# Softmax sums applied to the probabilities in SBUF, ahead of their transposes, in an AdaLN block with attention and experts

## What is computed

```python
e = jnp.exp(logits - m)
exp_sink = jnp.exp(s - m)
w = e / (jnp.sum(e, axis=-1, keepdims=True) + exp_sink)
out = jnp.einsum('bhmqk,bkhd->bqhmd', w, v).reshape(Bv, Tv, N_HEADS * HEAD_DIM)
return out @ out_w.T + out_b
```

## Time and profile before

| | us |
|---|---|
| median of 3 runs | 1054.87 (1053.17 to 1055.72) |
| profiled execution | 1054.14 |
| its span, first to last instruction | 1052.6 |
| TensorE busy, by matmuls | 957.0 |
| VectorE busy | 752.4 |
| ScalarE busy | 745.2 |
| GpSimd busy | 466.5 |
| mean granted TensorE clock | 0.963 of full speed |

### The profile page before, as it was taken

The page is one execution under the profiler, slowest core; times in us unless marked ns, Lnnn a source line. Parts: engine busy times, 40 slices in busy tenths (PEclk is TensorE's granted clock), DMA queues, the critical chain, the costliest instruction groups (busy, mean ns, idle before and its releaser), DMA issues.

```text
span 1052.6 us, 22639 instructions
## 1 busy us (share of the span) xinstructions
PE 957.0 (91%) x6862; PEld 897.0 (85%) x6862; DVE 752.4 (71%) x2212; ACT 745.2 (71%) x2058; POOL 466.5 (44%) x551
## 2 busy tenths in 40 slices
PE   5689999999899899999999999999997599999991
PEld 3479899989789799988999999999996489999991
DVE  6677887878788467777777777777764756666646
ACT  3368787888788688788878788887885356565541
POOL 4347668768657333433443332222222852222243
PEclk9889999999999899999999999999998699999996
DMA  8789879698467576465556555444302375555313
GB/s 183 176 221 280 219 209 272 209 216 206 116 162 170 160 192 158 114 167 134 136 142 166 132 150 137 116 120 152 81 2 96 115 263 161 175 163 163 104 59 117
DMA packets 146040, 166.09 MB, mean 158 GB/s; under 512 B 79194, under 2 KB 100714, under 8 KB 140800
## 3 DMA queue, kind: packets, MB, share of 16 engines
q1 hardware_dynamic: 129440, 143.58, 51.9%
q0 software_dynamic: 3696, 11.09, 3.3%
q10 hardware_dynamic: 12784, 9.97, 3.1%
HBM read 105.82 MB, written 58.79 MB: 156 GB/s over the span
## 4 chain that ended last, share of the span: by engine, by line
PE 63%; DVE 13%; ACT 9%; issue 8%; DMA 3%; POOL 2%; SPq 1%; ACTq 0%; DVEq 0%; POOLq 0%
PE psO L1107 15%; PE psS L1074 11%; PE psX L1084 9%; PE psY L1123 7%; PE psP L1003 7%; ACT wgt_hi L1340 3%; DVE gated L2094 2%; PE psO L1090 2%; PE psP L1016 2%; PE psP L1033 2%; POOL xg L910 2%; DVE pTl L1776 1%; ACT relu_s L1636 1%; PE psS L1257 1%; PE psX L1257 1%
## 5 line engine op out<-in xcount | busy, mean ns | idle before, releaser
L1372 ACT ACTIVATE pbuf<-pbuf,nmax 128x257 f32<-128x257 f32 (+5 forms) x512 | 264.2, 518 | 45.0 <-DVE nmax L1750 36.7
L1074 PE MATMUL psS<-kT,qE 128*128 128x256 f32 (+3 forms) x1024 | 237.2, 316 | 24.2 <-DVE nmax L1750 13.8
L1776 DVE TENSOR_TENSOR pTl<-psX,pTh 128x512 fp32r<-128x512 f32 x272 | 187.1, 688 | 71.4 <-ACT pTh L1340 70.4
L1340 ACT ACTIVATE pTh<-psX 128x512 fp32r<-128x512 f32 x272 | 160.6, 590 | 58.8 <-PE psO L1107 41.5
L1074 PEld LDWEIGHTS psS<-kT,qE 128*128 128x128 f32 x1024 | 161.2, 192 | 35.7 <-DVE nmax L1750 22.0
L1107 PE MATMUL psO<-pTh,vpad 128*128 128x256 f32 x1088 | 186.3, 293 | 3.3 <-DVE oS L1782 2.1
L814 POOL TENSOR_TENSOR ol<-oS,oh 128x256 fp32r<-128x256 f32 x128 | 94.8, 741 | 201.5 <-ACT oh L1340 197.0
L1084 PE MATMUL psX<-idn,pbuf 128*128 128x128 f32 x1088 | 161.8, 274 | 2.7 <-DVE pTl L1776 2.6
L1107 PEld LDWEIGHTS psO<-pTh,vpad 128*128 128x128 f32 x1088 | 149.7, 189 | 10.6 <-DVE oS L1782 5.5
L1753 DVE CUSTOM_DVE_ANT_0 pbuf<-psS,mcau 128x128 f32<-128x128 f32 (+3 forms) x256 | 123.0, 484 | 24.7 <-PE psS L1074 22.7
L1750 DVE CUSTOM_DVE_ANT_0 pbuf<-psS,mcau 128x257 f32<-128x257 f32 (+1 forms) x256 | 98.8, 387 | 50.3 <-PE psS L1074 47.0
(11 more groups left out here) (294 smaller groups left out, 2359.7 us busy)
## 6 DMA issues: line engine op xcount, KB each, us to landing
qd<-st SPq DMA_DIRECT2D x32, 1024.0 KB, 4.5
qE<-qd SPq DMA_DIRECT2D x128, 256.0 KB, 5.9
mrawV<-in_w_moe SPq DMA_DIRECT2D x32, 384.0 KB, 3.5
mrawB<-in_w_moe SPq DMA_DIRECT2D x32, 384.0 KB, 3.4
kT<-kd SPq DMA_DIRECT2D x64, 128.0 KB, 4.3
kT<-kd SPq DMA_DIRECT2D x32, 256.0 KB, 4.3
kd<-st SPq DMA_DIRECT2D x7, 1024.0 KB, 5.5
xg<-sq ACTq DMA_DIRECT2D x7, 640.0 KB, 6.2
```

Source lines behind the costliest of these rows:

```text
L1074: last = mm(psS[j % 2][:, at:at + n], qE[:, g % 2, j, t * P:(t + 1) * P], kT[:, g % 2, c, k0:k0 + n], start=(c == 0), stop=(c == 1))
L1340: copy = lambda o, i: nc.scalar.activation(o, i, ACT.Copy)
L1372: nc.scalar.activation(pj, pj, ACT.Exp, bias=nmax[:, u % 4, j:j + 1], scale=-1.0, accum_out=sums[:, u % 4, j:j + 1]).then_inc(a_exp, 1)
L1776: V.tensor_tensor(pTl[:, kt % 2, :], psX[kt % 2][:, :], pTh[:, kt % 2, :], ALU.subtract).then_inc(v_pl, 1)
```

## The change

The four heads' probabilities are multiplied with their reciprocals in SBUF, in place in `pbuf`, before TensorE turns them: heads 0 and 1 by one instruction of GpSimd, head 2 on VectorE, head 3 on ScalarE. The first `turn_probs` of a unit waits for all three in place of the exponentials. `spread`, `turn_scale`, `scale_of` and `scale_out` go, and with them `rdenx`, `rS` and `oS`. `oh` is now rounded from `psO` itself, `ol` is taken by VectorE from `psO` too, and `values` of the next unit waits for that. The reciprocals are made one step earlier (`denominator(u - 1)` in step u), the products stand in step u+1 of each engine, and `out_project` comes one step earlier. On GpSimd, `rope_low`, `low_weights`, the product and `rope_sum` now come in this order at the head of a step, ahead of `tables` and `residual`.

```diff
+
+        def heads_of(u):
+
+            n = keys(u) * P
+            step = n + 2 if windowed(u) else n
+            at = PROB[u % TB]
+            return pbuf[:, at:at + 2 * step].rearrange("p (j n) -> p j n", j=2)[:, :, step - n - windowed(u):step - windowed(u)]

...

-            def out_low(u):
-                pool.wait_ge(a_oh, u + 1)
+            def normalize(u):
+
+                pool.wait_ge(v_rden, u + 1)
                 apart(pool)
-                G.tensor_tensor(ol[:, u % 2, :], oS[:, u % 2, :], oh[:, u % 2, :], ALU.subtract).then_inc(g_ol, 1)
-
-            def spread(u):
-
-                pool.wait_ge(v_rden, u + 1)
-                wait(pool, s_rx, u)
-                apart(pool)
-                G.tensor_copy(rdenx[:, :].rearrange("p (h d) -> p h d", h=QM),
-                              rden[:, u % 4, :].unsqueeze(2).broadcast_to([P, QM, HD])).then_inc(g_rx, 1)
+                both = heads_of(u)
+                G.tensor_tensor(both, both, rden[:, u % 4, 0:2].unsqueeze(2).broadcast_to([P, 2, keys(u) * P]), ALU.mult)\
+                 .then_inc(g_norm, 1)

...

             def step(u):
                 seg, r = divmod(u, SEGU)
-                if 0 <= u - 4 < NU:
-                    out_low(u - 4)
+                if turns(u - 1):
+                    rope_low(ahead(u - 1)[:2])
+                if u < NU:
+                    low_weights(u)
+                if 0 <= u - 1 < NU:
+                    normalize(u - 1)
+                if turns(u):
+                    rope_sum(ahead(u)[:2])
                 if seg == 2 and 8 <= r < 20:
                     tables(r - 8)
                 if seg in (1, 2) and 3 <= r < 3 + TB:
                     residual(TB * (seg - 1) + r - 3)
-                if turns(u - 1):
-                    rope_low(ahead(u - 1)[:2])
-                if u < NU:
-                    low_weights(u)
-                if turns(u):
-                    rope_sum(ahead(u)[:2])
-                if 0 <= u - 1 < NU:
-                    spread(u - 1)
...
@@ -1078,22 +1075,18 @@
             def turn_probs(u, k):
                 kt = KT[u] + k + 1
                 if k == 0:
-                    pe.wait_ge(a_exp, QM * (u + 1))
+                    pe.wait_ge(g_norm, u + 1)
+                    pe.wait_ge(v_norm, u + 1)
+                    pe.wait_ge(a_norm, u + 1)
                 wait(pe, v_pl, kt - 2)
                 for j in range(QM):
                     last = turn(psX[kt % 2][:, j * P:(j + 1) * P], probs(u, j)[:, k * P:(k + 1) * P], idn[:, :])
                 last.then_inc(s_X, 1)

-            def turn_scale(u):
-                pe.wait_ge(g_rx, u + 1)
-                for i in range(2):
-                    last = turn(psO[:, (2 + i) * P:(3 + i) * P], rdenx[:, i * P:(i + 1) * P], idn[:, :])
-                last.then_inc(s_rx, 1)
-
             def values(u, k):
                 kt = KT[u] + k + 1
                 if k == 0:
-                    wait(pe, v_os, u)
+                    wait(pe, v_ol, u)
...
@@ -1138,11 +1131,9 @@
                 if u >= 3:
                     values(u - 3, keys(u - 3) - 1)
                 scores(u, 1)
-                if u >= 3:
-                    turn_scale(u - 3)
                 scores(u, 2)
-                if u >= 5:
-                    out_project(u - 5)
+                if u >= 4:
+                    out_project(u - 4)
                 scores(u, 3)
...
                 if nk > 3:
                     turn_probs(u - 2, 3)
-                out_project(u - 5)
+                if u - 4 < NU:
+                    out_project(u - 4)
...

-            def scale_of(u):
-                act.wait_ge(s_rx, u + 1)
-                wait(act, v_os, u - 1)
-                copy(rS[:, u % 2, :], psO[:, 2 * P:4 * P]).then_inc(a_rx, 1)
-
             def out_hi(u):
-                act.wait_ge(v_os, u + 1)
+                act.wait_ge(s_PV, KT[u + 1])
                 wait(act, s_Y, u - 1)
-                copy(oh[:, u % 2, :], oS[:, u % 2, :]).then_inc(a_oh, 1)
+                copy(oh[:, u % 2, :], psO[:, 0:2 * P]).then_inc(a_oh, 1)
+
+            def normalize(u):
+
+                act.wait_ge(v_rden, u + 1)
+                pj = probs(u, QM - 1)
+                nc.scalar.activation(pj, pj, ACT.Copy, scale=rden[:, u % 4, QM - 1:QM]).then_inc(a_norm, 1)

...
                 exp_head(u, 0)
-                if u >= 3:
-                    scale_of(u - 3)
                 if nk > 1:
                     probs_hi(u - 2, 1)
-                if u >= 4:
-                    out_hi(u - 4)
+                if u >= 3:
+                    out_hi(u - 3)
                 exp_head(u, 1)
+                if u >= 1:
+                    normalize(u - 1)
                 exp_head(u, 2)
                 if item and by_scalar(item):
                     high(item)
...
                 if u - 3 < NU:
-                    scale_of(u - 3)
+                    out_hi(u - 3)
                 if now:
                     exp_head(u, 1)
                 if nk > 1:
                     probs_hi(u - 2, 1)
+                if u - 1 < NU:
+                    normalize(u - 1)
                 if now:
                     exp_head(u, 2)
...
                     exp_head(u, 3)
-                if u - 4 < NU:
-                    out_hi(u - 4)
...

-            def scale_out(u):
-                dve.wait_ge(s_PV, KT[u + 1])
-                wait(dve, g_ol, u - 1)
-                dve.wait_ge(a_rx, u + 1)
-                V.tensor_tensor(oS[:, u % 2, :], psO[:, 0:2 * P], rS[:, u % 2, :], ALU.mult).then_inc(v_os, 1)
+            def normalize(u):
+
+                dve.wait_ge(v_rden, u + 1)
+                pj = probs(u, 2)
+                V.tensor_scalar(pj, pj, rden[:, u % 4, 2:3], None, ALU.mult).then_inc(v_norm, 1)
+
+            def out_lo(u):
+                dve.wait_ge(a_oh, u + 1)
+                V.tensor_tensor(ol[:, u % 2, :], psO[:, 0:2 * P], oh[:, u % 2, :], ALU.subtract).then_inc(v_ol, 1)

...
                 mask_max(u, 0)
-                if u >= 2:
-                    denominator(u - 2)
+                if u >= 1:
+                    denominator(u - 1)
                 mask_max(u, 1)
                 mask_max(u, 2)
+                if u >= 1:
+                    normalize(u - 1)
                 if nk > 0:
                     probs_lo(u - 2, 0)
                 next_sinks(u, 0)
-                if u >= 3:
-                    scale_out(u - 3)
                 if nk > 1:
                     probs_lo(u - 2, 1)
+                if u >= 3:
+                    out_lo(u - 3)
                 one_tile(u)
                 mask_max(u, 3)
...
                 if now:
                     mask_max(u, 0)
+                if u - 1 < NU:
+                    denominator(u - 1)
+                if now:
                     mask_max(u, 1)
                 if nk > 0:
                     probs_lo(u - 2, 0)
                 if now:
                     mask_max(u, 2)
                 if u - 3 < NU:
-                    scale_out(u - 3)
-                if u - 2 < NU:
-                    denominator(u - 2)
+                    out_lo(u - 3)
+                if u - 1 < NU:
+                    normalize(u - 1)
                 if nk > 1:
                     probs_lo(u - 2, 1)
```

More of the change, by code:

```diff
@@ L228, in build @@
         pTl = sb_att("pTl", [P, 2, QM * P], F32R)
-        rdenx = sb_att("rdenx", [P, QM * HD])
-        rS = sb_att("rS", [P, 2, 2 * P])
-        oS = sb_att("oS", [P, 2, 2 * P])
+        biasrow = sb_att("biasrow", [33, NKV * HD])
         oh = sb_att("oh", [P, 2, 2 * P], F32R)
         ol = sb_att("ol", [P, 2, 2 * P], F32R)
-        biasraw = oS[0:33, :, :].rearrange("p c n -> p (c n)")
+        biasraw = biasrow[:, :]
         wmod_s = pbuf[:, 0:KC * NMOD].rearrange("p (k n) -> p k n", k=KC)
@@ L390, in build @@
         v_rden = sem("v_rden")
+        v_norm = sem("v_norm")
+        a_norm = sem("a_norm")
+        g_norm = sem("g_norm")
+        v_ol = sem("v_ol")
         v_sink = sem("v_sink")
         v_pl = sem("v_pl")
-        v_os = sem("v_os")
         v_ye = sem("v_ye")
@@ L425, in build @@
         g_pl = sem("g_pl")
-        g_ol = sem("g_ol")
-        g_rx = sem("g_rx")
         s_mod = sem("s_mod")
@@ L434, in build @@
         s_Y = sem("s_Y")
-        s_rx = sem("s_rx")
-        a_rx = sem("a_rx")
         s_ht = sem("s_ht")
@@ L1113, in out_project @@
                 seg, t, g = u // SEGU, u % TB, u // TB
-                pe.wait_ge(g_ol, u + 1)
+                pe.wait_ge(v_ol, u + 1)
                 if t == 0:
@@ L1164, in step_causal @@
                     scores(u, 2)
-                if u - 3 < NU:
-                    turn_scale(u - 3)
                 if nk > 1:
@@ L1222, in _ @@
             pe.wait_ge(v_pl, KT[NU])
-            pe.wait_ge(v_os, NU)
+            pe.wait_ge(v_ol, NU)
             for t in range(TB, NT):
```

## The result

The changed kernel takes 1148.9 us (1148.0 to 1151.4), 1.0899 times the time before (95% interval 1.0881 to 1.0917). Its profiled execution has a span of 1146.6 us, 94.0 more than before.

What follows compares the result with a forecast made beforehand. TensorE's issue per unit was taken as the bound. From 1054.1 us: -28 transposes, +8 small delays, +102 waits behind `rope_low`, +34 slow clock, -8 old wait, +108 in all, so 1162, stated as 1160; range 1100 to 1195.

Steps and rivals of the forecast that it cites:

- Waits behind `rope_low`: At 17 windowed units TensorE's transposes wait for GpSimd's product, queued behind `rope_low`: 4.9 to 7.0 us each, together 102 us.
- The clock: TensorE's granted clock falls to half after each of the 17 waits: 2 us each, 34 us, bounds 0 and 51.
- Transposes: TensorE loses two transposes of spread reciprocals per unit, 0.22 us of issue: 28 us less over 128 units.
- what TensorE issues per unit sets the time: In both halves of attention TensorE is the bound, busy 96 and 99.7 us of 100.
- Small delays: ScalarE's product and VectorE's earlier reciprocal delay perhaps a third of windowed units by 0.1 to 0.8 us: +8 us.
- The old wait: TensorE's existing long wait between 346 and 351 us goes: 5 us of waiting and 3 of slow clock, -8 us.
- Causal half: The causal half of attention (550 to 650 us lies in it) becomes shorter by about 14 us.
- the second rival: VectorE's products wait behind GpSimd instructions at the shared SBUF port: +30 us in 47 windowed units, 1190 us; chance 0.12.
- Six microseconds hold 2.4 us of GpSimd with room: In the causal half GpSimd's product, up to 2.4 us, fits between the reciprocal and TensorE's transposes.
- room on VectorE: Argument against the port rival: VectorE has 22 of 100 us free in the windowed half.
- The first rival: Product's wait hidden or short, removed transposes decide: 1034, up to 1045 us; needs delay per pair under 1.2 us; chance 0.07.

Runs made afterwards that it cites:

- product_first: Changed kernel with GpSimd's product moved ahead of the rope subtractions and low weights in each step: 1063.8 us, ratio 1.0083 to the kernel before.
- keep_pe_awake: Changed kernel with 34 extra identity transposes on TensorE inside each of the 17 waits: 1128.2 us, ratio 1.0683 to the kernel before.
- scale_turned_once: Kernel before the change, with only the first of the two reciprocal transposes made from unit 1 on: 1042.8 us, ratio 0.9886.
- after_scalar_two: Changed kernel, its GpSimd order kept, with heads 2 and 3 both divided on ScalarE and none on VectorE: 1145.5 us, ratio 1.0872.
- the best version: Changed kernel with GpSimd's product first, rope sums behind it, and heads 2 and 3 both divided on ScalarE: 1043.5 us, ratio 0.9907.
- sum_behind: Changed kernel with GpSimd's product ahead of rope subtractions and low weights, and the rope sums moved behind it: 1053.5 us, ratio 1.0003.

## Why the prediction was right

1160 was predicted, 1148.9 measured, inside 1100 to 1195 and slower, as forecast; in span +108 against +94.0. The largest term and its cause were right, and they carry the result. That the sum came so close owes something to luck, as the misses on the other terms partly cancel. Term by term, with the forecast's numbers in front:

- **Waits behind `rope_low`: 102 forecast, 93.7 measured** (3.7 to 6.9 us each; unit 17: 6.3 as forecast, unit 26: 3.7 where 5.0 was). The number, 17, the units and the releasing instruction are as forecast, and product_first proves the cause. The size missed for two reasons. The product costs 1.05 us at 512 elements, not the 1.30 taken from a subtraction of two full operands; that is about 17 x 0.25 = 4 us. And TensorE itself comes later: at unit 26 its pair of scores is held 0.97 us by VectorE first, and from about 256.4, where its transposes could have begun, to the end of the two subtractions it is 2.6 us, where it was 3.7 in the earlier trace rows.
- **The clock: 34 forecast, between 21 (measured by keep_pe_awake, a lower bound) and 32 (the estimate there).** 2 us per wait was somewhat high. That half clock would follow each wait, as it did in the earlier trace rows, held for all 17. The Trainium skill (TensorE: Matmul & The Clock Gate, "HAM oscillation — how this bites in real kernels") describes this pattern of a throttle paid again at each gap; the trace agrees, with 17 stretches at half at 17 waits.
- **Transposes: -28 forecast, -19 to -24 measured**, by doubling and halving. The step that failed is that all of it lies on the path ("what TensorE issues per unit sets the time"): in the windowed half a pair is worth 0.10 to 0.17 us per unit, not 0.22.
- **Small delays: +8 forecast, -3 to +8 left over in units 0 to 63** (+106.1 - 1.7 = 104.4 measured there; 93.7 of waits, 21 to 32 of clock, -8 for the old wait and about -10 for transposes make 97 to 108). This is a remainder and carries the errors of all the others. The trace speaks against the term: outside the 17 waits TensorE's weight loads stand idle 13.7 us in units 0 to 52, and 19.8 before.
- **The old wait: -8 forecast.** It is gone: no wait of the scores for a maximum of more than 0.3 us stands in this part, where there had been one of 5.1. That the forecast had its cause right fits product_first, where without the new wait at unit 52 one of 4.1 us is back. Units 53 to 63 are only 1.7 us shorter since they hold that new wait (5.4 us); without it they would be some 7 us shorter, 1.4 to 3.6 of them for the transposes.
- **Causal half: 14 us shorter forecast, 5.5 measured.** The transposes give 12 there (scale_turned_once, twice 5.8) and 5.2 are lost to VectorE's held product (after_scalar_two). Sign right. The missing term is the mechanism of the second rival, in the half for which the forecast had found room enough ("Six microseconds hold 2.4 us of GpSimd with room"), and the low weights ahead of the product made it as large as it is.
- **Not forecast:** the part behind the last unit is 6.5 us shorter. Before, TensorE's last output projection ended 24.5 us behind the first scores of unit 127, now 21.0, since it is made at a distance of four units, not five, and one projection fewer is left for the end. That is 3.5 us; the other 3 stay open, and among the runs with the change this part varies from 263.6 to 267.9 us.

**The rivals.** The second, the shared port, is real: VectorE's product takes up to 1.9 us where it needs 0.5. It did not decide, and the reason was not the one I gave (room on VectorE). It hid behind the larger wait in the windowed half; once that was taken away, VectorE's product was worth 11 us there. The Trainium skill (SBUF — State Buffer, "Who interferes with whom") says that `tensor_scalar` in a two-port mode and GpSimd lock each other out for a whole instruction. The runs here agree for this form, fp32 in SBUF: 0.48 us free, 1.82 us as the median when started inside GpSimd's product (512 columns). The first rival set its threshold right: with the waits at 1.2 us each (product_first, 20.6 / 17) the change is within 1% of nothing. It assumed that 1034 would follow, and no version of the change that I ran came under 1043.

What stays open: in the best version units 0 to 52 still take 7.4 us more than before, although the transposes saved 5 to 9 there. That is about what TensorE waits more: its weight loads stand idle 35.5 us in this part, and 19.8 before. Waits of up to 3.3 us stand at many units, 19.1 us in sum outside the 17, put down to GpSimd's product or to issue. ScalarE is at 88 us of 100 in that stretch, and the longest wait, at unit 40, ends with ScalarE's product by the matmuls' row. But sum_behind, where ScalarE has one product and not two, already has 14.4 us of such waits and the long one at unit 40, so ScalarE's second product makes at most a part of them.

## What to carry to other kernels

When a step is moved to an engine ahead of a consumer that issues in order, write down what stands in front of it in that engine's queue and what each of those waits for. Here the product cost 1 us and its place in the queue about 4.5, seventeen times, plus a slower clock behind each. Put what the bound engine needs next at the head of the step, and the rest behind it: that alone turned a ratio of 1.090 into 1.008. A second cost can be covered by the first one; repair the large wait before you call a suspected conflict harmless. And the price of a conflict depends on the order: VectorE's same product cost 5.2 us of the causal half in one order of GpSimd's queue and 1.2 in the other.

## What the runs showed of the hardware

- A GpSimd product with a broadcast second operand is cheaper than one of two full operands: 616, 1046, 1467 and 1897 ns at 256, 512, 768 and 1024 elements, against 741, 1313 and 1828 ns at 256, 512 and 768 in subtractions. That it is the operand and not the operation shows at 256: the one multiplication of two full fp32 operands (L826 of the changed kernel) takes 758 ns, 738 as the median.
- VectorE's `tensor_scalar`, fp32 from SBUF to SBUF, takes 0.28, 0.34, 0.41 and 0.48 us at 128, 256, 384 and 512 columns when GpSimd is idle. The 0.51 us at 256 in the earlier trace rows, from which I priced it, is well over that. When it starts inside a GpSimd product, sum or subtraction, it ends 0.08 to 0.3 us behind that one, or, six times in the changed kernel, behind the rope sum that follows at once (L806, started inside L805); it takes up to 1.9 us. GpSimd's products show none of it: 1.03 to 1.10 us at 512 nearly always (one 1.22).
- Waits of 3.7 to 6.9 us on TensorE each brought 3.4 to 10.2 us of granted clock at half, and this cost 1.2 us of time per wait as measured, 1.9 by the highest estimate (21 and 32 us for 17).
